# Parts of queries and keys brought to the heads' rows by 0/1 matmuls, and heads kept in halves of a tile

## The reference

```
NL, D, H, DFF = (6, 128, 16, 512)          # head width 8
def _attn(q, k, v, mask):
    scores = einsum('bqhd,bkhd->bhqk', q, k) / sqrt(HD)
    scores = where(mask, -inf, scores)
    return einsum('bhqk,bkhd->bqhd', softmax(scores), v)
for i in range(NL):
    xn = adaln(x, n1);  q, k, v = split(xn @ qkv_w[i].T)
    x = x + _attn(rope(q), rope(k), v, src_mask) @ so_w[i].T
    xn = adaln(x, n2);  q = rope(xn @ cq_w[i].T)
    x = x + _attn(q, rope(context @ ck_w[i].T), context @ cv_w[i].T, ctx_mask) @ co_w[i].T
    xn = adaln(x, n3)
    x = x + gelu(xn @ f1_w[i].T + f1_b[i]) @ f2_w[i].T + f2_b[i]
```

## Time and profile before

| | us |
|---|---|
| median of 3 runs | 4610.91 (4610.57 to 4612.44) |
| profiled execution | 4613.32 |
| its span, first to last instruction | 4611.5 |
| transformer stage within it, preparation included | about 2049 to 3605 |
| mean granted clock of TensorE | 0.91 |

### The profile page before, as it was taken

One profiled execution on the slowest core, in us unless ns is written; L12 is line 12 of the kernel. 1 busy time (PEld: TensorE's weight loads), 2 busy tenths in 40 slices (PEclk: granted clock), 3 DMA queues, 4 the chain that ended last, 5 costly groups with the idle time before them and its releaser, 6 DMA issues. The chain is left out here.

```text
span 4611.5 us, 83547 instructions
## 1 busy us (share of the span) xinstructions
PE 4031.0 (87%) x24597; PEld 2622.9 (57%) x24597; DVE 3249.7 (70%) x16939; ACT 2277.7 (49%) x7483; POOL 407.0 (9%) x338
## 2 busy tenths in 40 slices
PE   8999999999999999876888888888887346979897
PEld 6888888888888888653333333333333223644456
DVE  7888888888888888665666666666664455456543
ACT  5555555555555555432655555555555222236432
POOL 0000000000000000011111111111111010024310
PEclk9999999999999999886988888888888667989998
DMA  0000000000000000012122222222220002500001
GB/s 30 2 2 2 2 2 2 2 2 2 2 2 2 2 2 2 15 43 69 27 50 54 50 54 50 54 50 54 49 51 17 5 4 72 139 30 6 11 10 42
DMA packets 92091, 121.98 MB, mean 26 GB/s; under 512 B 28292, under 2 KB 75583, under 8 KB 91396
## 3 DMA queue, kind: packets, MB, share of 16 engines
q1 hardware_dynamic: 91651, 116.82, 10.0%
HBM read 85.42 MB, written 30.53 MB: 25 GB/s over the span
## 5 line engine op out<-in xcount | busy, mean ns | idle before, releaser
L297 DVE CUSTOM_DVE_ANT_0 I-197junk<-I-193encw,I-196expo,I-205rec 128x77 f32<-128x77 f32 x3072 | 945.6, 356 | 7.0
L1335 DVE TENSOR_REDUCE I-41263nmax<-ps 128x1 f32<-128x512 f32 x768 | 500.9, 686 | 201.8 <-PE ps L1003 192.0
L1223 ACT ACTIVATE I-41266prob<-ps 128x512 f32<-128x512 f32 x768 | 428.4, 595 | 238.1 <-PE ps L1040 235.5
L275 ACT ACTIVATE I-195tanh_s<-ps 128x77 f32<-128x77 f32 x1024 | 241.3, 236 | 594.9 <-PE ps L255 594.9
L255 PEld LDWEIGHTS ps<-I-190hist,I-49small 128*128 128x128 f32 x2048 | 304.6, 188 | 298.3 <-DVE I-190hist L333 298.3
L255 PE MATMUL ps<-I-190hist,I-49small 128*128 128x77 f32 x2048 | 456.4, 304 | 0.2
L261 PE MATMUL ps<-I-195tanh_s,I-49small 128*128 128x77 f32 x2048 | 454.6, 304 | 0.0
L262 PE MATMUL ps<-I-190hist,I-49small 128*128 128x128 f32 x2048 | 439.5, 296 | 0.0
L257 PE MATMUL ps<-I-190hist,I-194uh_h 128*128 128x128 f32 x2048 | 439.5, 296 | 0.0
L283 ACT ACTIVATE I-201hh<-I-207gate_t,I-206pre,I-200rh 128x1 f32<-128x1 f32 x1024 | 395.5, 386 | 88.0 <-DVE I-206pre L297 0.2
L1003 PE MATMUL ps<-I-41257kS,I-41256qS 96*128 96x512 bf16 x768 | 346.2, 470 | 83.0 <-DVE I-41263nmax L1335 58.0
(11 more groups left out here) (542 smaller groups left out, 7062.9 us busy)
## 6 DMA issues: line engine op xcount, KB each, us to landing
I-41256qS<-parts SPq DMA_DIRECT2D x96, 192.0 KB, 4.9
parts<-I-41275room SPq DMA_DIRECT2D x36, 384.0 KB, 2.5
parts<-I-41275room SPq DMA_DIRECT2D x36, 256.0 KB, 2.1
I-41257kS<-parts SPq DMA_DIRECT2D x48, 192.0 KB, 4.6
I-61029spread<-gates_rows SPq DMA_DIRECT2D x24, 256.0 KB, 4.1
I-61030spread<-gates_rows SPq DMA_DIRECT2D x22, 256.0 KB, 4.1
I-61031spread<-gates_rows SPq DMA_DIRECT2D x22, 256.0 KB, 4.0
parts<-I-41275room SPq DMA_DIRECT2D x36, 128.0 KB, 1.8
```

The lines of the kernel that those rows point to most:

```text
L297: return e.tensor_tensor_reduce(junk[:, 2 * g + b, :], encw[:, g, b, :], expo[:, b, :], inv[:, b:b + 1], rec[:, b, g:g + 1], ALU.mult, ALU ...
L1223: e.activation(prob[:, tau % 2, j, :], k.ps[:, b, :], ACT.Exp, scale=scale).then_inc(free[b], 1)
L1335: e.tensor_reduce(nmax[:, U % HG, i, j:j + 1], k.ps[:, use[0], :], AX.X, ALU.max, negate=True).then_inc(free[use[0]], 1)
```

## The change

Two heads now share the columns of `qS`, `kS` and `cS` (`[128, B, 8, T]`): even heads have rows 0 to 63, odd heads rows 64 to 127 (`head`). Each half has the 48 rows of parts, the mask in row 48 and the maximum in rows 49 and 50. All maxima and score matmuls, also the cross ones, use the 64 rows of one half.

`place` replaces `store` and `spread`. For each pair of heads it makes four matmuls into one bank of the rest stream: one with two rows (`extra`, `fixed`) that brings mask and ones, and three with a matrix of zeros and ones (`pick`) that carry the three parts from `part3` to their rows. `keep_heads` copies the bank to the tile, ScalarE for even pairs, VectorE for odd ones. The two transfers of maxima rows stay. The cross maxima take their matmuls in another order, so that the four of one bank use the same half. The preparation fills `pick`, `extra` and `fixed` instead of the large tiles, and the mask row has memory of its own. The strings of `TURNS` are new for all engines and written out for the whole stage, with no repeated part.

```diff
+                    def place(name, n, w, at, m):
+                        for p in PAIRS:
+                            use = R[r, ("p", name, p)]
+                            b = open_bank(e, use)
+                            e.matmul(k.ps[:, b, 0:m], extra[:, w, :], fixed[:, at:at + m], start=True, stop=False, skip_group_check=True)
+                            for which, ready in enumerate((jhigh, middle, last)):
+                                if p == 0:
+                                    e.wait_ge(ready[n], job[r, name])
+                                mm = e.matmul(k.ps[:, b, 0:m], pick[:, w, p, which, :], part3[:, n, which, 0:m], start=False,
+                                              stop=(which == 2), skip_group_check=True)
+                            mm.then_inc(full[b], 1)
...
                             if n == 0:
-                                e.wait_ge(jsent["q"][m], 16 * (a + 1))
-                                e.wait_ge(jsent["k"][m], 16 * (a + 1))
+                                for p in (2 * m, 2 * m + 1):
+                                    e.wait_ge(*done(R[a, ("p", "q", p)]))
+                                    e.wait_ge(*done(R[a, ("p", "k", p)]))
...
-                            e.matmul(k.ps[:, b, :], qS[0:ROWS_QK, c, 4 * m + j, i * P:(i + 1) * P],
-                                     kS[0:ROWS_QK, c, 4 * m + j, :], start=True, stop=True,
+                            e.matmul(k.ps[:, b, :], head(qS, c, 4 * m + j)[:, i * P:(i + 1) * P],
+                                     head(kS, c, 4 * m + j), start=True, stop=True,
...
+                    def keep_heads(name, m, dst):
+                        for p in PAIRS[1::2]:
+                            use = R[r, ("p", name, p)]
+                            e.wait_ge(*made(use))
+                            e.tensor_copy(dst[:, c, p, :], k.ps[:, use[0], 0:m]).then_inc(free[use[0]], 1)
+                            yield
...
-                    if r < NA:
-                        yield from deliver("k", 0, T, kS, K_SPOTS)
-                        yield from deliver("q", 1, T, qS, Q_SPOTS)
```

Two lines of `TURNS` (the beginning of SyncE's string):

```diff
-    sync=("rrrrrrrrrrmrmrrrrrmrrmmrrrrrrrrrrmrrrrmmrrrrrrrrrrrrrrrmrrrrrrrmm",
+    sync=("rrrmmmrmmrmrrrmmrrmrrrrmmrmrmrrrrmmmrrmrrrrmmrmrmrrrrmmmrrmrrrrmmrmrmrrrrmmmrrmrrrrmmrmrmrrrrmmmrrmrrrrmmrmmrm"
```

272 lines of the change are left out of this document (147 added, 125 removed).

## The result

The changed kernel takes 4914.86 us (median of 4 runs, 4898.91 to 4927.64) against 4611.67 (4610.57 to 4613.62) of the kernel before: 1.0655 times as long, 95% interval 1.062 to 1.069. The prediction was 4580, with a range of 4505 to 4700; the time lies 335 us above the forecast and 215 above the upper end. The profiled execution took 4907.82 us.

What follows compares the result with a forecast made beforehand. TensorE was taken as the busiest engine, with a thin stretch held by transfers and queue order. From 4613.3 us, -29 (preparation) +6 +5 +5 (ends) -18 (period 121.6 to 120) gave 4582, stated as 4580, range 4505 to 4700.

Steps and rivals of the forecast that it cites:

- thin stretch: 35 us of each unit's period, 59 matmuls at clock 0.60; most of its 19 us cross-maxima wait put to SyncE's queue order.
- Part 1: Preparation: the last modulation load no longer waits for fills, so the modulation matmuls start earlier; -29 us (-31 to -24).
- Part 2: TensorE work per unit: 82.5 us plus placements and shape changes, less 10.9 for overlapping halves; 104 us, or 115 without overlap.
- Part 3: Copies out of the banks: 8 us a unit on ScalarE, 9 on VectorE; given no term of its own.
- Part 4: Transfers replaced by placements: shorter waits and later projection nearly cancel; the gain is placements in empty time at full clock.
- I leave it 13: Loss kept in the dense stretch of each period, which lost 15 of 86 us before.
- I leave it 3: Loss kept in the thin stretch of each period for the norm chain; it lost 24 of 35 us before.
- The dense one: The other 86 us of each period, with 501 matmuls at clock 0.98; it lost 15 us.
- The ends: Ends of the stage: opening +6, first unit's dense stretch +5, last cross placements +5 us.
- (a): Rival: TensorE becomes the bound as halves overlap half or not at all; 4646 or 4710 us, chance 0.37.
- almost no waits: Sign for the rival with TensorE as bound: TensorE shows almost no waits and units come 125 us apart.
- The sign of waits on VectorE: If TensorE waits for VectorE, the copies cost what the prediction put at nothing.

Runs made afterwards that it cites:

- swap: Kernel before with the preparation changed, plus SyncE issuing the cross-query reload ahead of a maxima-row send from the third layer on; 4585.87 us.
- full_bare: Changed kernel with 128 rows everywhere, placements without 0/1 matmuls, their remaining matmul and copies cut to 8 columns; 4580.5 us.
- full_rows: Changed kernel with 128 rows in each placement's first matmul and in all maxima and score matmuls; 4722.81 us.
- wide_extra: Changed kernel with the two-row first matmul of each placement widened to 128 rows, 126 of them zeros; 4780.74 us.
- full_no_pick: full_rows with all three 0/1 matmuls of every placement left out, only the matmul for mask and ones left; 4652.6 us.
- the preparation alone: Kernel before with only the preparation changed: mask row in its own place, last modulation load sent with the others; 4585.21 us.

## Why the prediction was wrong, step by step

**What bounds the kernel.** Right that TensorE's queue does, wrong in what makes the thin stretch thin. I took it for transfers and SyncE's order. The run swap shows maxima at VectorE's pace ahead of the cross maxima, and full_bare that without the transfers, in the new order, the kernel gains 5 us. The 82.5 us of work before were right: the table has 83.3, changes included.

**Part 1** was right: -29 us predicted, -27.3 us in the start of the modulation matmuls, and 29.6 us less alone than the kernel before beside it on the same chip (4614.84).

**Part 2, the work**, was sized well. I had 104 us with changes of shape; the table has 92.3 + 16.8 = 109.1. Overlap gave 7 to 8 us instead of 10.9 (the work of full_rows less that of wide_extra is 6.9). The count of pairs was about right: 53 a unit start within 0.02 us of each other. But only 37 of them are two matmuls of 512 columns (31 maxima or scores); the others hold a cross maximum of 77 columns and save little, where I priced all 52 at a full spacing. The Trainium skill ("TensorEngine Tiling (Array Packing)", Key Properties) has different tiles execute in parallel, and here the trace now agrees for row halves.

**Part 3, the copies**, at nothing: nearly right. All of them cost 7 us in full_rows; in the changed kernel half of them cost 25 us, with overlapping runs. With the 0/1 matmuls gone (full_no_pick) they cost 65.

**Part 4 and the period: the step that failed** is "I leave it 13" and "I leave it 3", 16 us of idle time and low clock a period in place of 39. Measured are 17.2 + 21.5 = 38.7, as much as before (10.4 + 27.2 = 37.6). The added work was to lie "in time that was empty, and at the full clock", and "that stretch should not fall to 0.60". Its mean clock over the nine periods is 0.67, and in the unit shown 20 us of it ran at 0.50. In sum nothing of the idle time was used up, and the period is the old one plus the added work and changes: 121.6 + 109.1 - 83.3 = 147.4, against 148.9.

Between the two stretches it went as follows (the same split, coarser for small matmuls, so that its terms add up to within 4 us of the table's). The thin one was to hold 30 us of work and to lose 3; it holds 17 and loses 15, 8 to the clock and 7 to waits (before: 8 and 23). The dense one was to hold 74 us and to lose 13; it holds 88 and loses 27, 10 to the clock and 17 to waits (before: 73 and 16). So the thin stretch has about the length that I gave it, and gave up 8 us of its waits; the dense one is 29 us longer than forecast. The premise that failed with the step is that the placements lie in time that was empty. Seven placements of q between the last score and the projection's end, on which part 4 is built, stand there only in units 5 to 8; in units 3 and 4 there are three, in all others none. The time from the last score to the projection's end is accordingly 14.9 us in those four units (13 predicted) and 7.9 to 8.7 in the others but the last.

Why so, by the runs, from the preparation alone to the changed kernel (each difference of medians; 11 periods):

| step | us | a period |
|---|---|---|
| transfers, order, waits (full_bare) | -5 | -0.4 |
| the last matmul of a placement | +7 | 0.6 |
| three 0/1 matmuls | +128 | 11.7 |
| copies | +7 | 0.6 |
| halves instead of 128 rows | +58 | 5.3 |
| two rows instead of 128 in the first matmul | +134 | 12.2 |
| sum | +330 | |

Each price holds with the other parts as they stand in that pair of runs: the copies cost 7 us here and 65 without the 0/1 matmuls. The column divides by 11 and so holds the ends of the stage too. The 0/1 matmuls alone are hidden by a quarter (128 of 177 us), where I had them hidden whole. The halves were to return 10.9 - 4.4 us a period and cost 5.3: in the table changes (6.4) take back what the overlap returns (6.9), and the low clock adds 6.9. The two-row matmul was counted with 0.19 us, 6 us a period, and cost 12.2; in the table it is 11.1, with 4.9 of changes, 7.4 of clock and 1.7 less of waits.

**The ends** were to give +16 and gave some +39. The opening gave +11 (16.4 us earlier instead of 27.3) where I had 6; nine of its sixteen placements ran at the low clock. The first unit gave +20 where I had 5 (its projection ends 3.4 us later than before, after a first maximum 16.4 us earlier), and the end of the stage +8 where I had 5.

**Rivals.** (a), TensorE as the bound, comes nearest, but its two prices, 4646 and 4710, rested on the share of 0.87. The work of its first price, 109 us, is what was measured; the share was 109.1 / 148.9 = 0.73. What the case lacked is the low clock and the waits, and its sign of "almost no waits" did not come: there are 21.5 us of them. The sign of waits on VectorE came, but what it was to show, dear copies, did not. VectorE's maxima are the largest single part of TensorE's idle time in the changed kernel, 49 of 117 us over the eight units, as before (44 of 141). Groups over eight units (busy us, mean ns | idle before, what ended it):

```profile
L1392 DVE TENSOR_REDUCE I-41266nmax<-ps 128x1 f32<-128x512 f32 x519 | 336.4, 684 | 148.1 <-PE ps L1032 145.8
L1032 PE MATMUL ps<-I-41257kS,I-41256qS 64*128 64x512 bf16 x519 | 175.1, 434 | 53.8 <-DVE I-41266nmax L1392 48.6 <-ACT I-55xh L1284 4.2 <-ACT I-41278room L1344 0.4
```

The first row says that VectorE waits for TensorE 146 us, the second that TensorE waits for VectorE 49: each for the other in turn, over two banks.

## What to carry to other kernels

Idle time of an engine that works a fixed order is not a place for new work until it is shown what ends each wait, and that the new work stands at that place in every unit: an order written out without a repeated part has to be counted unit by unit. A stripped version (full_bare) tells early what a change can win at most in the new order, here 5 us. If an engine's clock depends on what it does, a form with fewer rows can cost more than it saves: price it at both clocks, and look at what stands next to it. A small matmul of another shape (two rows) was as dear as the three 0/1 matmuls beside it (134 and 128 us), and 126 rows of zeros took its price away.

## What the hardware showed that I had not expected

TensorE can be busy without a gap and stay at 1.2 GHz: 50.8 us of 64-row matmuls, 53.5 us of 64 and 128 rows in turn, 20 us in the changed kernel itself. The same matmuls in both halves at once have a mean clock of 0.91 over 18.8 us. Started at the full clock, 120 of the 64-row matmuls kept it to their end, for some 26 us. The Trainium skill ("TensorE: Matmul & The Clock Gate", Part 1: The HAM clock gate) lets the clock depend on how busy TensorE has been; these rows differ from that, since all of these streams were equally busy, and the measurement decides. Where the line lies between rows that lift it and rows that do not, the runs don't say.

What stays open: what the low clock costs by itself, since no run changed it alone; the split puts 14.3 us a period of it between the changed kernel and full_rows, with 2.6 us more waits. Open is also why a quarter of the 0/1 matmuls is hidden and not more, and why in the kernel the clock falls inside the dense stretch: the streams show what does not lift it, not what lets it fall.
